# A graph recommender on one core: SyncE and ScalarE gather row by row one tile in two rounds instead of one in each

## The chip, the cores and the metric

The kernel runs on one core of a Trainium2 chip. The metric is the device time of one execution in microseconds, the median over several runs; lower is better. The engines are TensorE (PE), VectorE (DVE), ScalarE (ACT), GpSimd (POOL) and SyncE (SP), each with its own instruction queue; they meet by semaphores.

## The reference, cut to what matters

The graph has 12,501 nodes with rows of 128 float32 (`emb`) and 150,000 edges (row, column, value).

```python
h = emb
acc = emb
for _ in range(2):
    h = segment_sum(adj_val[:, None] * h[adj_col], adj_row, num_segments=N)
    acc = acc + h
graph_item_embs = acc / 3
combined = graph_item_embs[items] + item_features[items]
# 512 sessions of 50 items: gather through alias_inputs, two small products with tanh
# and sigmoid, a weighted sum per session, normalized: select (512 x 128)
scores = select @ l2norm(graph_item_embs).T          # 512 x 12501
```

The part around the change is `h[adj_col]`: for each of two layers, one row of 512 bytes is fetched from HBM for each edge.

## The kernel before, in words

**Sorting.** A first stage sorts the edges by buckets of 256 target nodes into a table in HBM (`sorted_edges`), padded so that each tile of 128 edges belongs to one bucket. There are NU = 1244 tiles.

**A layer.** For every tile, 128 rows of the source (`emb` in layer 0, `table1` in layer 1) are gathered into one slot of `msg`, one row per partition. VectorE writes a one-hot matrix of 128 x 256 with the edges' values (L1118), TensorE multiplies it with the gathered rows (L1444), and VectorE adds the result to the bucket's columns of `acc` in SBUF (L1167). The one-hot is made LEAD = 4 tiles ahead.

**Rounds.** The tiles go in rounds of T = 24: NST = 52 rounds, numbered c = 0 to 51, the last with 20 tiles. `msg` holds two rounds, h = c % 2. Before a round, ScalarE copies its 24 columns of metadata into small buffers (`fetch`, L660 to L662) once the matmuls of round c - 2 are done; the last of the copies releases GpSimd's gathers of that round.

**Who gathers.** GpSimd issues one indirect DMA for each tile (L574), in order of the tiles; at tiles 0, 8 and 16 of a round it waits until the matmul of 12 tiles earlier is done (PACE = 8, AHEAD = 12). The last tile of the rounds 1 to 49 (`is_own`, NOWN = 49 in each layer) is left out there: SyncE and ScalarE gather it row by row, 64 rows each. For each half of 32 rows they load 32 byte offsets into registers (L442, L682), and for each row issue one copy of 512 bytes (L446, L686), each with a MOVE before it. All 128 rows count on one semaphore (`s_line`), which VectorE waits for before the one-hot of that tile and then clears. The offsets stand in `own_at`, which VectorE prepares from the sorted edges before the layers.

**Order on ScalarE.** In layer 0, for each round: fetch(c), then its 64 rows of the last tile of round c. In layer 1: wait for TensorE's transposes of embeddings, two copies (L710, L711) that TensorE's next transposes (L1438) need, fetch(c + 2), then the 64 rows of round c + 2. On SyncE: a wait for the matmuls that free the slot, then the 64 rows.

**After.** Between the layers `acc` is transposed and written to HBM as `table1`; after layer 1 the session part follows, with 200 indirect gathers by GpSimd and the 512 x 12501 scores.

Of the kernel before, what the change touches and what calls it, by code (L numbers as in the profile page):

```python
# [38 lines left out]
def recommender_program(nc, items, inputs, alias, features, adj_row, adj_col, adj_val, emb,  # L39
# [34 lines left out]
    T = 24  # L74

    NT = -(-((E + GR * NB * (R - 1) + NB * (P - 1)) // P) // T) * T
    NST = NT // T
# [2 lines left out]
    PACE, AHEAD = 8, 12  # L80
    LINE = 4 * D
    HALF, AT_ONCE = P // 2, 32
    NOWN = NST - 3
    M = 4
    NU = -(-((E + GR * NB * (R - 1) + NB * (P - 1)) // P) // M) * M
    PER = NU // M
# [18 lines left out]
    FITS = "a tile's offset is 256 times the buckets that begin at or before it, less one: 0 to ROWS - 256"  # L105

    def is_own(j):
        return j % T == T - 1 and 1 <= j // T <= NOWN

    FED = [sum(1 for j in range(u, NU, 2 * T) if not is_own(j)) for u in range(2 * T)]  # L110

# [2 lines left out]
    with ExitStack() as ctx:  # L114
# [55 lines left out]
        at[0] = -(-NT // P) * 2 * P  # L170
        own_lines = carve(big, NOWN * HALF * 2)[0:2, :].rearrange("o (k s w) -> o k s w", k=NOWN, w=2)
        assert at[0] <= ROWS
# [57 lines left out]
        block_at_l = carve(stage, NKL * P)  # L230
        own_at = stage[0:2, 6 * D:6 * D + NOWN * HALF].bitcast(I32)
        assert 6 * D + NOWN * HALF <= 4 * 512 * 2
        assert at[0] <= 4 * 512 * 2
# [107 lines left out]
        s_lines = sem("s_lines")  # L341
# [4 lines left out]
        s_mm = [sem(f"s_mm{m}") for m in range(M)]  # L346
# [52 lines left out]
        emb_bytes = emb.rearrange("n d -> (n d)").bitcast(U8)  # L399
        table1_bytes = table1.rearrange("n d -> (n d)").bitcast(U8)  # L400
# [15 lines left out]
        @block.sync  # L416
        def _(sp):
            sp.wait_ge(s_init, 3)
            for n, (dst, src) in enumerate(((e_row, adj_row), (e_col, adj_col), (e_val, adj_val))):
                sp.dma_start(dst[:, 0:COLS], src[0:COLS * P].rearrange("(p t) -> p t", t=COLS)).then_inc(s_edge, 16)  # L420
                sp.dma_start(dst[0:TAIL, COLS:COLS + 1],
                             src[COLS * P:E].rearrange("(p t) -> p t", t=1)).then_inc(s_edge, 16)
            sp.wait_ge(s_blank, 2)
            sp.dma_start(slots.rearrange("(p x) w -> p (x w)", p=P), blank.rearrange("p x w -> p (x w)")).then_inc(s_zero, 16)

            sp.wait_ge(s_free, GR + 3)
            lines = slots.rearrange("(j x) w -> j (x w)", x=P // R)
            full = NT // P
            sp.dma_start(big[:, 0:2 * P], lines[0:P, :]).then_inc(s_meta0, 16)
            sp.dma_start(big[:, 2 * P:full * 2 * P].rearrange("p (m w) -> p m w", m=full - 1),  # L430
                         lines[P:full * P, :].rearrange("(m p) w -> p m w", p=P)).then_inc(s_meta, 16)
            sp.dma_start(big[0:NT - full * P, full * 2 * P:(full + 1) * 2 * P], lines[full * P:NT, :]
                         ).then_inc(s_meta, 16)
            for half in range(2):
                sp.dma_start(own_lines[half:half + 1].rearrange("o k s w -> o k (s w)"),
                             lines[T:T * (NOWN + 1), 2 * HALF * half:2 * HALF * (half + 1)
                                   ].rearrange("(k t) w -> t k w", t=T)[T - 1:T]).then_inc(s_lines, 16)

            def own_rows(source, first, h):

                for a in range(0, HALF, AT_ONCE):
                    _, starts = nc.values_load_multi_w_load_instructions(  # L442
                        own_at[0:1, bass.ds(first + a, AT_ONCE)], engines=[mybir.EngineType.SP],
                        min_val=0, max_val=LINE * (N - 1), skip_runtime_bounds_check_because=HELD)
                    for p, begin in enumerate(starts):
                        sp.dma_start(msg_bytes[h][a + p:a + p + 1, :],  # L446
                                     source[bass.ds(begin, LINE)].rearrange("(o b) -> o b", o=1)).then_inc(s_line[h], 16)

            def own_tiles(layer, source):

                own_rows(source, 0, 1)
                with sp.Fori(1, NST // 2 - 1) as i:
                    for h in range(2):
                        sp.wait_ge(s_mm[M - 1], i * (2 * T // M) + (PER * layer + T // M * (h - 1)))
                        own_rows(source, i * (2 * HALF) + HALF * (h - 1), h)

            sp.wait_ge(s_mrdy, 3)
            own_tiles(0, emb_bytes)

            for r in range(NB // GRP):  # L460
                sp.wait_ge(s_t1a, (GRP * (r + 1) + 1) // 2)
                sp.wait_ge(s_t1v, (GRP * (r + 1)) // 2)
                a, b = 2 * GRP * r, 2 * GRP * (r + 1)
                sp.dma_start(tab[0][:, a:b, :], big_rows[:, a:b, :]).then_inc(s_t1w, 16)
            sp.wait_ge(s_t1w, 16 * (NB // GRP))

            sp.dma_start(big_rows[:, 0:emb_full, :],
                         emb[0:emb_full * P, :].rearrange("(g p) d -> p g d", p=P)).then_inc(s_eld, 16)
            sp.wait_ge(s_fz, 1)
            sp.dma_start(big_rows[0:emb_rest, emb_full, :], emb[emb_full * P:N, :]).then_inc(s_eld, 16)  # L470

            own_tiles(1, table1_bytes)

            sp.wait_ge(s_ec, NB)
            sp.dma_start(big_rows[0:emb_rest, emb_full, :], features[emb_full * P:N, :]).then_inc(s_fld, 16)
            sp.dma_start(big_rows[:, 0:emb_full, :],
                         features[0:emb_full * P, :].rearrange("(g p) d -> p g d", p=P)).then_inc(s_fld, 16)
            for r in range(NB // GRP):
                sp.wait_ge(s_cmb, GRP * (r + 1))
                a, b = 2 * GRP * r, 2 * GRP * (r + 1)  # L480
                sp.dma_start(tab[1][:, a:b, :], ring_rows[:, a:b, :]).then_inc(s_cw, 16)

            for bt in range(BT):
                for q in range(-(-NS // 2)):
                    m = (-(-NS // 2)) * bt + q
                    sp.wait_ge(s_sca, m + 1)
                    if 2 * q + 1 < NS:
                        sp.wait_ge(s_scv, (NS // 2) * bt + q + 1)
                    a, b = 1024 * q, min(1024 * q + 1024, N)
                    sp.dma_start(out[bt * P:(bt + 1) * P, a:b], ostage[:, m % 4, 0:b - a]).then_inc(s_out[m % 4], 16)  # L490
            total = (-(-NS // 2)) * BT
            for i in range(4):
                sp.wait_ge(s_out[i], 16 * ((total - i + 3) // 4))
# [109 lines left out]
        def _(act):  # L603
# [63 lines left out]
            for m in range(-(-NT // P)):  # L667
                w = min(P, NT - P * m)
# [10 lines left out]
            def own_rows(source, first, h):  # L679

                for a in range(0, HALF, AT_ONCE):
                    _, starts = nc.values_load_multi_w_load_instructions(  # L682
                        own_at[1:2, bass.ds(first + a, AT_ONCE)], engines=[mybir.EngineType.Activation],
                        min_val=0, max_val=LINE * (N - 1), skip_runtime_bounds_check_because=HELD)
                    for p, begin in enumerate(starts):
                        act.dma_start(msg_bytes[h][HALF + a + p:HALF + a + p + 1, :],  # L686
                                      source[bass.ds(begin, LINE)].rearrange("(o b) -> o b", o=1)).then_inc(s_line[h], 16)
# [3 lines left out]
            with act.Fori(1, NST // 2 - 1) as i:  # L691
                for h in range(2):
                    fetch(0, 2 * i + h, h)
                    own_rows(emb_bytes, i * (2 * HALF) + HALF * (h - 1), h)
            for c in range(NST - 2, NST):
                fetch(0, c, c % 2)

# [15 lines left out]
            with act.Fori(0, LOOP // 2) as i:  # L713
                for h in range(2):
                    emb_rows(2 * i + h, h)
                    fetch(1, 2 * i + h + 2, h)
                    own_rows(table1_bytes, i * (2 * HALF) + HALF * (h + 1), h)
            for c in range(LOOP, max(NB, NST - 2)):
                if c < NB:
                    emb_rows(c, c % 2)  # L720
# [74 lines left out]
        def _(dve):  # L795
# [301 lines left out]
            for m in range(-(-NT // P)):  # L1097
                w = min(P, NT - P * m)
# [9 lines left out]

            def one_hot(layer, it, u):

                if u % T < T - 1:
                    dve.wait_ge(s_g[u], 16 * (FED[u] * layer + it + 1))
                elif isinstance(it, int) and not is_own(2 * T * it + u):
                    dve.wait_ge(s_g[u], 16 * (FED[u] * layer + (FED[u] if it else 1)))
                else:
                    dve.wait_ge(s_line[u // T], 16 * P)
                    dve.sem_clear(s_line[u // T])
                dve.tensor_scalar(onehot[:, u % SR, :], bank[7][:, 0:BUCKET], mlo[:, u:u + 1], mval[:, u:u + 1],  # L1118
                                  ALU.is_equal, ALU.mult).then_inc(s_S[u % M], 1)
# [469 lines left out]
```

## Time and profile before

| | us |
|---|---|
| median of 3 runs | 4178.22 |
| lowest, highest | 4175.29, 4179.51 |
| profiled execution, span | 6020.2 |
| busy in it: PE, DVE, POOL | 3070.2, 3014.4, 2890.1 |
| busy in it: PEld, ACT | 1849.5, 866.4 |

The profile shows one execution, with the hardware's recorder of instructions on; for it no time other than the span is given. Its span is 1842 us longer than the median of the runs, which are made without the recorder. Rows of the profile are those of this longer execution. Time that an engine's queue spends on issuing a DMA, on register moves and on loads of registers is not in its busy time; the rows name such a queue with a q (ACTq, SPq).

### The profile page before, as it was taken

To read this page: it belongs to the slowest core of one execution; us is meant where nothing else is said; L and a number is where in the kernel's file an instruction comes from. 1 tells how busy PE (TensorE), PEld (TensorE's weight loads), DVE (VectorE), ACT (ScalarE), POOL (GpSimd) and SP (SyncE) were. 2 spreads that over 40 slices of the span, in tenths; PEclk is the share of its full clock that TensorE was granted. 3 is DMA by queue.
4 is the path that set the end of the run, shared out by engine and by line. 5 is a ranking of instruction groups with operands and counts; after the bars stand their busy time and mean duration, and the time that the engine had idled before them with its cause. 6 is when DMAs were issued, how large, how long until landed. Compare 5 with 4: busy or idle time off the path is not lost.

```text
span 6020.2 us, 68764 instructions
## 1 busy us (share of the span) xinstructions
PE 3070.2 (51%) x9778; PEld 1849.5 (31%) x9778; DVE 3014.4 (50%) x7257; ACT 866.4 (14%) x3005; POOL 2890.1 (48%) x2965
## 2 busy tenths in 40 slices
PE   5988744444444444444444444444444444445578
PEld 3777622222222222222222222222222222222344
DVE  8999754444444444444444444444444444445455
ACT  2998800000000000000000000000000000000543
POOL 1666654444444444444445454454454454455561
PEclk8888866666666666666666666666666666666689
DMA  0000011111111111111114111111111111112454
GB/s 25 4 3 3 3 48 33 32 31 32 32 31 33 33 34 33 34 33 31 32 32 120 34 37 35 33 37 36 32 37 35 33 37 35 34 36 80 79 84 139
DMA packets 162229, 235.35 MB, mean 39 GB/s; under 512 B 67554, under 2 KB 107776, under 8 KB 161952
## 3 DMA queue, kind: packets, MB, share of 16 engines
q0 software_dynamic: 92896, 171.14, 12.4%
q1 hardware_dynamic: 54132, 58.90, 3.0%
q10 hardware_dynamic: 15052, 3.83, 0.3%
q14 instruction: 118, 0.97, 0.1%
q8 instruction: 31, 0.51, 0.0%
HBM read 192.69 MB, written 41.01 MB: 39 GB/s over the span
## 4 chain that ended last, share of the span: by engine, by line
ACTq 49%; issue 32%; DVE 7%; PE 6%; ACT 3%; another core or an unknown queue 2%; POOL 1%; DMA 0%; DVEq 0%; SPq 0%; POOLq 0%
ACTq L686 43%; ACTq L682 5%; ACT big L644 2%; PE bank L1520 1%; PE bank L1382 1%; POOL sorted_edges L542 1%; DVE stage L944 1%; PE bank L1548 1%; DVE acc L1167 1%; DVE big L888 1%; PE bank L1507 1%; DVE ring L896 0%; PE bank L1482 0%; DVE big L904 0%
## 5 line engine op out<-in xcount | busy, mean ns | idle before, releaser
L1444 PE MATMUL bank<-ring 128*128 128x256 f32 x4976 | 2105.7, 558 | 2135.8 <-DVE ring L1118 1194.1
L1444 PEld LDWEIGHTS bank<-ring 128*128 128x128 f32 x4976 | 1147.7, 263 | 3071.0 <-DVE ring L1118 1662.5
L574 POOL DMA_INDIRECT ring<-in_L_rec_emb,cring x1195 | 1134.9, 950 | 1336.2 <-ACT cring L662 978.9
L1167 DVE TENSOR_TENSOR acc<-acc,bank 128x256 f32 x2488 | 1029.6, 414 | 1481.3 <-remote 1131.6
L1118 DVE TENSOR_SCALAR ring<-bank,mlo,mval 128x256 f32<-128x256 f32 x2488 | 1343.5, 540 | 742.4 <-DMA ring<-in_L_rec_emb 523.1
L574 POOL DMA_INDIRECT ring<-table,cring x1195 | 1130.2, 946 | 1202.8 <-PE bank L1444 795.7
L644 ACT ACTIVATE big<-big 128x68 f32<-128x68 bf16 x1764 | 557.7, 405 | 1.2 <-issue 1.2
L1382 PE MATMUL bank<-big,ring 128*128 128x136 f32 x2352 | 430.8, 328 | 75.5 <-issue 20.8
L542 POOL DMA_INDIRECT sorted_edges<-moved,block_to x313 | 397.2, 1269 | 100.3 <-issue 100.0
L1382 PEld LDWEIGHTS bank<-big,ring 128*128 128x128 f32 x2352 | 356.8, 219 | 147.6 <-ACT big L644 83.2
L660 ACT COPY mlo<-ring 128x24 f32 (+1 forms) x104 | 21.7, 209 | 2415.0 <-issue 2381.6
L710 ACT COPY idle<-ones 128x1 f32<-128x1 f32 x49 | 9.4, 192 | 2191.6 <-issue 2191.6
L1438 PE MATMUL bank<-ident,stage 128*128 128x128 f32 x98 | 33.7, 448 | 524.7 <-ACT stage L711 524.7
L597 POOL DMA_INDIRECT ring<-combined,sidi x200 | 190.5, 952 | 156.6 <-issue 56.0
L1148 DVE TENSOR_TENSOR acc<-acc,bank 128x256 f32 (+1 forms) x49 | 20.6, 421 | 468.1 <-PE bank L1438 468.1
L1438 PEld LDWEIGHTS bank<-ident,stage 128*128 128x128 f32 x98 | 14.2, 204 | 556.9 <-ACT stage L711 556.9
L896 DVE TENSOR_TENSOR ring<-bank,place_p 128x1024 f32<-128x1024 f32 x147 | 178.7, 1215 | 7.0 <-remote 4.1
L1520 PE MATMUL bank<-acc,big 128*128 128x512 f32 (+1 forms) x200 | 104.7, 635 | 5.5 <-ACT big L754 3.5
L888 DVE TENSOR_TENSOR big<-bank,place_c 128x544 bf16<-128x544 f32 x147 | 105.4, 717 | 0.3
L1391 PE MATMUL bank<-dsnow,ring 50*128 50x1 f32 x626 | 98.6, 288 | 0.0
L1391 PEld LDWEIGHTS bank<-dsnow,ring 50*128 50x128 f32 x626 | 96.9, 244 | 2.5
L904 DVE TENSOR_TENSOR big<-big 128x272 f32<-128x272 bf16 x147 | 92.8, 632 | 0.0
(213 smaller groups left out, 1700.7 us busy)
## 6 DMA issues: line engine op xcount, KB each, us to landing
ring<-in_L_rec_emb SPq DMA_DIRECT2D x3136, 0.5 KB
ring<-in_L_rec_emb ACTq DMA_DIRECT2D x3136, 0.5 KB
ring<-table ACTq DMA_DIRECT2D x3136, 0.5 KB
ring<-table SPq DMA_DIRECT2D x3136, 0.5 KB
scores<-stage SPq DMA_DIRECT2D x48, 512.0 KB
ring<-in_L_rec_emb,cring POOLq DMA_INDIRECT x1195
ring<-table,cring POOLq DMA_INDIRECT x1195
table<-big SPq DMA_DIRECT2D x7, 896.0 KB, 9.1
```

Of the source, the lines that this page charges most:

```text
L542: pool.indirect_dma_start(slots, bass.IndirectOffsetOnAxis(block_to[:, h, k:k + 1], 0), moved[:, h, (skip + k) * R:(skip + k + 1) * R, :]. ...
L574: pool.indirect_dma_start(msg[:, s, :], None, source, bass.IndirectOffsetOnAxis(cring[:, s:s + 1], 0)).then_inc(s_g[s], 16)
L597: pool.indirect_dma_start(seq[:, half, l, :], None, combined, bass.IndirectOffsetOnAxis(sidi[:, l, bt:bt + 1], 0)).then_inc(s_sq[half * NG ...
L644: last = act.activation(at_c[:, r, t, q, :], hot_c[:, r, :, t], ACT.Copy, scale=what[:, bass.ds(n * C + t, 1)])
L682: _, starts = nc.values_load_multi_w_load_instructions(own_at[1:2, bass.ds(first + a, AT_ONCE)], engines=[mybir.EngineType.Activation], mi ...
L686: act.dma_start(msg_bytes[h][HALF + a + p:HALF + a + p + 1, :], source[bass.ds(begin, LINE)].rearrange("(o b) -> o b", o=1)).then_inc(s_li ...
L896: dve.tensor_tensor(at_p[:, r, :, :], row_p.unsqueeze(1).broadcast_to([P, C, P]), place_p[:, h, s * C:(s + 1) * C].unsqueeze(2).broadcast_ ...
L1118: dve.tensor_scalar(onehot[:, u % SR, :], bank[7][:, 0:BUCKET], mlo[:, u:u + 1], mval[:, u:u + 1], ALU.is_equal, ALU.mult).then_inc(s_S[u ...
L1167: add = dve.tensor_tensor(acc[:, bass.ds(off, BUCKET)], acc[:, bass.ds(off, BUCKET)], bank[u % PR][:, 0:BUCKET], ALU.add)
L1382: last = pe.matmul(group_bank(h)[:, 0:2 * LC], at_p[:, r, t, :], at_c[:, r, t, :, :].rearrange("p w c -> p (w c)"), start=(s == 0 and t == ...
L1391: last = pe.matmul(bank[7][:, k:k + 1], begun[0:NB + 1, k * P:(k + 1) * P], dsnow[:, :], start=True, stop=True)
L1444: pe.matmul(bank[u % PR][:, 0:BUCKET], msg[:, h * T + u, :], onehot[:, u % SR, :], start=True, stop=True).then_inc(s_mm[u % M], 1)
```

## The change

The row-by-row tile becomes the last tile of every second round: tiles 47, 95, ... in place of 47, 71, 95, .... NOWN goes from 49 to 25 in each layer; the rounds 1, 3, ..., 49 keep theirs, and the last tiles of the rounds 2, 4, ..., 48 are gathered by GpSimd like all others. The loops of SyncE and ScalarE issue their 64 rows once for two rounds, after the fetch of the odd one, and always into the slot of h = 1. VectorE's wait for the other slot's last tile becomes the ordinary one. `FED`, which counts GpSimd's gathers per slot, follows from `is_own`.

```diff
-    NOWN = NST - 3
+    NOWN = NST // 2 - 1
...
     def is_own(j):
-        return j % T == T - 1 and 1 <= j // T <= NOWN
+        return j % (2 * T) == 2 * T - 1 and j // (2 * T) < NOWN
...
                 sp.dma_start(own_lines[half:half + 1].rearrange("o k s w -> o k (s w)"),
-                             lines[T:T * (NOWN + 1), 2 * HALF * half:2 * HALF * (half + 1)
-                                   ].rearrange("(k t) w -> t k w", t=T)[T - 1:T]).then_inc(s_lines, 16)
+                             lines[0:2 * T * NOWN, 2 * HALF * half:2 * HALF * (half + 1)
+                                   ].rearrange("(k t) w -> t k w", t=2 * T)[2 * T - 1:2 * T]).then_inc(s_lines, 16)
...
                 own_rows(source, 0, 1)
                 with sp.Fori(1, NST // 2 - 1) as i:
-                    for h in range(2):
-                        sp.wait_ge(s_mm[M - 1], i * (2 * T // M) + (PER * layer + T // M * (h - 1)))
-                        own_rows(source, i * (2 * HALF) + HALF * (h - 1), h)
+                    sp.wait_ge(s_mm[M - 1], i * (2 * T // M) + PER * layer)
+                    own_rows(source, i * HALF, 1)
...
             with act.Fori(1, NST // 2 - 1) as i:
                 for h in range(2):
                     fetch(0, 2 * i + h, h)
-                    own_rows(emb_bytes, i * (2 * HALF) + HALF * (h - 1), h)
+                own_rows(emb_bytes, i * HALF, 1)
...
                 for h in range(2):
                     emb_rows(2 * i + h, h)
                     fetch(1, 2 * i + h + 2, h)
-                    own_rows(table1_bytes, i * (2 * HALF) + HALF * (h + 1), h)
+                own_rows(table1_bytes, i * HALF + HALF, 1)
...
             def one_hot(layer, it, u):
 
-                if u % T < T - 1:
+                if u < 2 * T - 1:
                     dve.wait_ge(s_g[u], 16 * (FED[u] * layer + it + 1))
```

## Rows read from the trace of the kernel before

**Rows 1.** The page: span, busy time, DMA queues, chain that ended last

```profile
span 6020.2 us, 68764 instructions
...
PE 3070.2 (51%) x9778; PEld 1849.5 (31%) x9778; DVE 3014.4 (50%) x7257; ACT 866.4 (14%) x3005; POOL 2890.1 (48%) x2965
...
q1 hardware_dynamic: 54132, 58.90, 3.0%
q10 hardware_dynamic: 15052, 3.83, 0.3%
...
ACTq L686 43%; ACTq L682 5%; ACT big L644 2%; PE bank L1520 1%; PE bank L1382 1%; POOL sorted_edges L542 1%; DVE stage L944 1%; PE bank L1548 1%; DVE acc L1167 1%; DVE big L888 1%; PE bank L1507 1%; DVE ring L896 0%; PE bank L1482 0%; DVE big L904 0%
```

**Rows 2.** Timeline of ScalarE: start us, us, what; stalled, clean, second layer

```profile
3073.15 25.99 ACTq L686 DMA_DIRECT2D ring<-in_L_rec_emb  x12
...
3104.38 10.35 ACTq L686 DMA_DIRECT2D ring<-in_L_rec_emb  x32
3114.93 0.21 ACT L660 COPY mlo<-ring 128x24 f32 x1 [48.49 <-issue]
3115.05 0.21 ACT L661 COPY mval<-ring 128x24 f32 x1
3115.16 0.20 ACT L662 COPY cring<-ring 128x24 int32 x1
...
4537.02 1.19 ACTq L686 DMA_DIRECT2D ring<-table  x4
4538.25 0.19 ACT L710 COPY idle<-ones 128x1 f32<-128x1 f32 x1 [43.80 <-issue]
4538.36 0.41 ACT L711 COPY stage<-big 128x256 f32 x1
...
4541.08 9.65 ACTq L686 DMA_DIRECT2D ring<-table  x21
```

**Rows 3.** Lines 686, 682, 446 in short stretches: ns min/median/max, first and last

```profile
L686 ACTq MOVE ring<-in_L_rec_emb x12: 4/353/692, 3072.4 to 3097.7; - x12
...
L686 ACTq MOVE ring<-in_L_rec_emb x30: 29/29/29, 3104.3 to 3113.8; - x30
L686 ACTq DMA_DIRECT2D ring<-in_L_rec_emb x30: 228/229/462, 3104.4 to 3113.9; - x30
...
L682 ACTq TENSOR_LOAD <-stage x1: 2148/2148/2148, 3102.1 to 3102.1; - x1
...
L446 SPq MOVE ring<-in_L_rec_emb x13: 632/691/708, 3071.8 to 3098.4; - x13
L446 SPq DMA_DIRECT2D ring<-in_L_rec_emb x12: 5/694/701, 3072.4 to 3097.7; - x12
...
L446 SPq DMA_DIRECT2D ring<-in_L_rec_emb x3136: 3/225/1399, 775.5 to 3165.8; - x196
```

**Rows 4.** Timeline of GpSimd across the end of round 49, first layer

```profile
3138.15 0.94 POOL L574 DMA_INDIRECT ring<-in_L_rec_emb,cring  x1 [0.30 <-issue]
...
3143.15 0.94 POOL L574 DMA_INDIRECT ring<-in_L_rec_emb,cring  x1 [0.30 <-issue]
3163.84 0.95 POOL L574 DMA_INDIRECT ring<-in_L_rec_emb,cring  x1 [19.75 <-ACT cring L662]
```

**Rows 5.** Waits, whole span: us in total, times, longest us

```profile
POOL ring L574 <- ACT cring L662: 978.9, 50, 20.8
...
PE bank L1438 <- ACT stage L711: 524.7, 49, 15.9
```

**Rows 6.** Timeline of VectorE, nothing late: first and last of five tiles

```profile
3051.75 0.54 DVE L1118 TENSOR_SCALAR ring<-bank,mlo,mval 128x256 f32<-128x256 f32 x1
...
3055.66 0.54 DVE L1118 TENSOR_SCALAR ring<-bank,mlo,mval 128x256 f32<-128x256 f32 x1
```

**Rows 7.** Timeline of GpSimd: first gather, between the layers, last gather

```profile
756.38 0.98 POOL L574 DMA_INDIRECT ring<-in_L_rec_emb,cring  x1 [4.38 <-ACT cring L662]
...
3222.23 0.95 POOL L574 DMA_INDIRECT ring<-in_L_rec_emb,cring  x1 [0.30 <-issue]
3262.57 0.95 POOL L574 DMA_INDIRECT ring<-table,cring  x1 [39.38 <-DMA table<-big]
...
5555.23 0.95 POOL L574 DMA_INDIRECT ring<-table,cring  x1 [0.30 <-issue]
```

## The prediction, made before the changed kernel was run

> **What bounds the kernel now.** I started from the engines' busy times and the chain that ended last [rows 1]. The reader is to see two things. No engine is over 51% busy, and the chain lies 43% on L686 and 5% on L682, which are ScalarE's queue issuing single rows. And the span, 6020.2 us, is 1842 us longer than the 4178.22 us that the runs without the recorder take. A page that is 44% too long can name a bound that the timed runs don't have, so the first question is where the 1842 us lie.
>
> The views of ScalarE's queue answer it. In one stretch a half of 32 rows goes out in 10.35 us [rows 2] with its load of 2.15 us before it [rows 3]; in another, some 30 us earlier, 12 rows take 25.99 us [rows 2], a MOVE of a register between them takes up to 0.69 us where it otherwise takes 0.029, and SyncE's MOVEs and DMAs take 0.69 us in the same stretch [rows 3]. A MOVE issues no transfer. When it stretches on two engines at once, the thing that is slow is not the row transfer; I take it for the recording of the instructions, which the timed runs don't do. The pitch without these stalls is (10.35 - 0.46) / 31 = 0.319 us a row, 0.46 being the longest issue, the first after the load [rows 2, 3].
>
> From that follows ScalarE's round without stalls: a half is 2.15 + about 0.09 + 10.35 = 12.6 us, two are 25.2, and the fetch takes 3115.36 - 3114.73 = 0.63 us plus some 0.2 of the loop: 26.0 us a round [rows 2, 3]. In the second layer two more copies (L710, L711) come before the fetch: 4541.08 - 4538.21 = 2.87 us from row to row, load included, instead of 2.15 + 0.09 = 2.24, and the two copies are 0.1 to 0.4 us long; I take 26.4 there [rows 2]. SyncE has the same 64 issues, with 0.225 us in place of 0.229 each, and no fetch [rows 3].
>
> GpSimd gives the other side. Its gathers come at 1.251 us (3143.15 - 3138.15 over 4 steps), 0.95 us busy and 0.30 of gap, and then it waits 19.75 us for the fetch that ScalarE's stalled queue holds back [rows 4]. Without that wait a round of 23 gathers is 23 x 1.251 = 28.8 us. That is 2.4 to 2.8 us more than ScalarE's clean round. The rest is faster: VectorE turns a tile over in 0.78 us when nothing is late (3055.66 - 3051.75 over 5 tiles), 18.8 us a round [rows 6].
>
> Check by the sum. Outside the two gather stages lie 756.4 us before the first gather, 39.1 us between the layers (the 39.38 less the ordinary 0.30), and 6020.2 - 5555.2 - 1.25 = 463.7 us at the end: 1259.2 us [rows 1, 7]. With GpSimd as the only bound the kernel takes 1259.2 + 2 x 1195 x 1.251 = 4249 us. With ScalarE's clean rounds as the only bound it takes 1259.2 + 49 x 26.0 + 49 x 26.4 + 170 (two times 68 gathers of rounds that have no row-by-row tile) = 3997 us. The median of 4178.22 lies 181 us above the second and 71 us under the first, and 71 us is just 0.030 us per gather. So I read the timed runs as bound by GpSimd at (4178.2 - 1259.2) / 2390 = 1.221 us per gather, with the recorder costing the other 0.03. The difference in level is taken up by this: the span itself is no base for the sum, the median is.
>
> **The change part by part.**
>
> *Gathers added.* Row-by-row tiles fall from 49 to 25 in each layer, so GpSimd issues 24 more gathers per layer, 48 in all: 1195 become 1219 twice. Each is a gather on the engine that I hold for the bound. From below it costs 0.95 us (only the busy part, if the gap could be covered), from above 1.251 us (the pitch seen); I take 1.221. Sum: 48 x 1.221 = +58.6 us, bounds +45.6 and +60.0.
>
> *Row transfers removed.* 24 x 64 x 2 = 3072 issues go from each of SyncE and ScalarE, with 96 loads of 2.15 us. That frees ScalarE about 24 x 25.2 = 605 us per layer. It is worth nothing if its round lay 2 us under GpSimd's. The cover that hides it today is the row of gathers; if that cover is missing, the freed time is the gain of the first rival.
>
> *Lateness of the rows that stay.* They are issued after the fetch of the odd round, which waits on the same matmuls that free the slot, nearly two rounds before the tile is turned over. Clean, 25.2 us of issues stand against some 50 us. Behind them in ScalarE's queue stand the next fetch and, in the second layer, the copies L710 and L711, for which TensorE's transposes (L1438) wait. Today that is so every round, hereafter every second; it costs nothing new. In the profiled execution the queue will still stall, so some of TensorE's wait for L711 will be seen there.
>
> *Set-up.* The list of row addresses shrinks from 49 x 64 to 25 x 64; the three small VectorE steps on it (L1105 to L1107) get a few us shorter while GpSimd already gathers. They lie on nothing that ends last: taken as 0, with at most 5 us gained. VectorE's wait on the line semaphore and its clearing fall away 48 times in all and are replaced by the ordinary wait: 0.
>
> *Fewer transfers in flight.* The two hardware queues together, with everything else on them, take 3.3% of the DMA engines' span [rows 1], and GpSimd's gap of 0.30 us is the same beside rows in flight and after the last of them [rows 4, 7]. Taken as 0.
>
> **A rule that speaks for a gain.** ScalarE's issue is 0.229 us in the rows [rows 3]. The Trainium skill, page "DMA: Bandwidth & Descriptors", in the table that closes the section "Why a DMA increments its semaphore by 16 and not by 1", gives 512 sequencer cycles for a copy instruction of the earlier generations, and "Advanced Engine Details and Errata", section "Clock Domains", 1.2 GHz for the sequencers: 0.427 us each. By that rule, as an estimate, ScalarE's round would be 64 x 0.427 + 2 x 2.24 + 0.8 = 32.6 us, more than GpSimd's, the kernel before would take over 4600 us and the change would bring it down to the gathers' time. The trace does not agree: 0.229 us stands against 0.427, and the median of before is far under 4600. Its result is B below, in a stronger form.
>
> **The rivals.**
>
> *A, likeliest: GpSimd is the bound.* 1259.2 + 2438 x 1.221 = 4236.8, or 4178.2 + 58.6: **4237 us**. Chance 0.86. Own range 4215 to 4245, from the bounds of the price, the set-up, and the spread of the three runs (4.2 us).
>
> *B: ScalarE's queue bounds the timed runs too.* It needs (4178.2 - 1259.2 - 170) / 98 = 28.05 us a round, 2 us over the clean one, which is 0.03 us more per row than the trace's best. Then the gather pitch is unknown and lies somewhere under 1.221. The change is a gain from the point where it is under (4178.2 - 1259.2) / 2438 = 1.197 us. The recorder's share would be the one thing that makes the pitch smaller: if three recorded steps of 0.03 us were in a gather, it would be 1.16 us, and the time 1259.2 + 2438 x 1.16 = 4087 us. For it: the chain, and GpSimd's 978.9 us of waits for ScalarE [rows 1, 5]. Against it: the MOVEs of 0.69 us, and that 71 us fit one such step per gather. Chance 0.08.
>
> *C: both queues about equal.* Between them, with a gather of 1.19 to 1.20 us in the timed runs, gain and loss cancel: 1259.2 + 2438 x 1.197 = 4178 us. The two rounds are 2.4 us apart in the rows, which leaves room for it only if each is off. Chance 0.04.
>
> *D: a new wait.* In the second layer TensorE waits for L711 until ScalarE has issued a full tile (524.7 us of waits, with the stalls [rows 5]). Should the pile-up of one tile in every second round reach GpSimd's gathers (which stop when the matmuls lag by more than 12 to 20 tiles), 24 waits of 1 to 2 us come on top: 4260 to 4285, say 4272. Clean, the copies are due about 30 us after the issues begin, and a lag of under 10 us reaches no gather. Chance 0.02.
>
> **How the numbers follow.** Slower by over 0.2% (8 us, about what a measurement of this kernel can tell from no change) is A and D: 0.88. Same is C with a little of B: 0.04. Faster is B: 0.08. The range 4212 to 4248 holds about 0.93 of A and nothing of the others, 0.80 in all; it is A's own range, drawn a little wider.
>
> **What the profile of the changed kernel would show.** GpSimd with 1219 gathers twice and at the same 0.95 us; rows issued 1600 times per engine and layer; GpSimd's waits for the fetch nearly gone and the chain on GpSimd's gathers (or their gaps) instead of L686. Its span should fall far, to 1259 + 2438 x 1.251 = 4309 us plus what stalls are left, say 4310 to 4450, though the timed runs get slower. A median under 4170 would mean that the timed runs were bound by ScalarE's issues, and that the fastest pitch in the trace is not the pitch without the recorder. A median over 4250 would point to waits that the gathers run into.

## The result, and the profile after

The changed kernel takes **4235.46 us** (median of 4 runs, 4233.24 to 4237.0) against 4177.4 us (4 runs, 4175.29 to 4179.51): 58.1 us or 1.4% more, ratio 1.014 with the 95% interval 1.0126 to 1.0155. The forecast was 4237 us, slower.

The page of the changed kernel (its lines are one lower than those of before from L574 on: GpSimd's gather is L573, ScalarE's row L685, TensorE's product L1443):

```profile
span 4235.2 us, 56068 instructions
...
PE 3245.6 (77%) x9778; PEld 1823.8 (43%) x9778; DVE 3090.9 (73%) x7257; ACT 870.0 (21%) x3005; POOL 2928.7 (69%) x3013
...
q10 hardware_dynamic: 8908, 2.25, 0.3%
...
POOL ring L573 26%; POOL ring L596 2%; DMA scores<-stage 2%; PE bank L1519 1%; PE bank L1481 1%; PE bank L1547 0%; DMA ring<-table,cring 0%; PE bank L1472 0%; DMA ring<-combined,sidi 0%; PE bank L1506 0%; ACT stage L731 0%; ACT acc L725 0%; DMA table<-big 0%; PE bank L1488 0%; ACT big L742 0%
```

Beside [rows 1] the reader is to see that ScalarE's queue has left the chain and GpSimd's gathers are its largest part, and that this span, 4235.2 us, agrees with the timed runs, while the first profile of before is 1842 us above its own. A comparison of the two pages would call this change a gain of 30%.

The groups of the gathers, with what ended GpSimd's idle time before them, in the changed kernel:

```profile
L573 POOL DMA_INDIRECT ring<-in_L_rec_emb,cring x1219 | 1152.4, 945 | 376.0 <-issue 370.9 <-ACT cring L661 4.5 <-PE bank L1443 0.6
L573 POOL DMA_INDIRECT ring<-table,cring x1219 | 1150.2, 944 | 403.6 <-issue 369.6 <-DMA table<-big 32.1 <-PE bank L1443 1.8
```

GpSimd waits 4.5 us for ScalarE instead of the 978.9 of [rows 5], and nothing else of size but the wait for the table between the layers interrupts it. That is one engine at its own pace for 3046 us of 4235.

**The same kernel before, profiled again.** Because the first profile of before didn't fit its times, the unchanged kernel was profiled once more, and two further profiles with the same number of instructions came by the way (e2 and e3, below).

> The kernel before, unchanged, profiled once more. If the 6020 us of its first profile belong to the kernel under the recorder, the span is again near 6020 us, with MOVEs of up to 0.7 us on SyncE and ScalarE. If they belonged to that one execution, the span is 4171 to 4179 us as in the profiles of the runs that issue the same number of instructions (68764), with a pitch of 1.25 us for GpSimd's gathers and ScalarE waiting 2 to 3 us a round for the matmuls.

Measured: span 4178.4 us, time 4180.22 us. Its page, the gathers, and ScalarE's rows between 900 and 2200 us:

```profile
span 4178.4 us, 68764 instructions
...
POOL ring L574 24%; DMA ring<-table,cring 3%; PE bank L1520 2%; POOL ring L597 1%; DMA scores<-stage 1%; DMA ring<-combined,sidi 1%; PE bank L1444 1%; PE bank L1548 1%; PE bank L1482 1%; PE bank L1507 0%; DVE ring L1118 0%; PE bank L1473 0%; PE bank L1489 0%; ACT stage L732 0%; ACT acc L726 0%
```

```profile
L574 POOL DMA_INDIRECT ring<-in_L_rec_emb,cring x1195 | 1135.1, 950 | 369.2 <-issue 355.3 <-PE bank L1444 9.5 <-ACT cring L662 4.4
L574 POOL DMA_INDIRECT ring<-table,cring x1195 | 1130.1, 946 | 396.9 <-issue 354.3 <-DMA table<-big 32.2 <-PE bank L1444 10.4
```

```profile
L686 ACTq MOVE ring<-in_L_rec_emb x2816: 29/29/29, 901.0 to 2161.9; - x188
L686 ACTq DMA_DIRECT2D ring<-in_L_rec_emb x2816: 228/229/542, 901.0 to 2162.0; - x188
```

The long MOVEs of [rows 3] are not there, nor is the wait of [rows 4]. The 6020 us were those of one execution. Neither the kernel as such nor the recording of it takes that long. This profile is the one that the changed kernel's is to be compared with.

GpSimd's timeline at the ends of the stages, kernel before (again) and changed kernel:

```profile
742.98 0.99 POOL L574 DMA_INDIRECT ring<-in_L_rec_emb,cring  x1 [4.40 <-ACT cring L662]
...
2241.88 0.94 POOL L574 DMA_INDIRECT ring<-in_L_rec_emb,cring  x1 [0.31 <-issue]
2275.06 0.94 POOL L574 DMA_INDIRECT ring<-table,cring  x1 [32.23 <-DMA table<-big]
...
3768.91 0.95 POOL L574 DMA_INDIRECT ring<-table,cring  x1 [0.30 <-issue]
```

```profile
743.09 0.98 POOL L573 DMA_INDIRECT ring<-in_L_rec_emb,cring  x1 [4.45 <-ACT cring L661]
...
2266.02 0.94 POOL L573 DMA_INDIRECT ring<-in_L_rec_emb,cring  x1 [0.30 <-issue]
2299.09 0.94 POOL L573 DMA_INDIRECT ring<-table,cring  x1 [32.13 <-DMA table<-big]
...
3819.78 0.94 POOL L573 DMA_INDIRECT ring<-table,cring  x1 [0.30 <-issue]
```

With one pitch of 1.25 us for the last gather, the stages last 1500.2 + 1495.1 = 2995.3 us before and 1524.2 + 1521.9 = 3046.1 us after: 50.8 us more. Start (743.0 and 743.1) and the time between the layers are equal; the part after the last gather is 408.3 and 414.2 us. It varies between 405.7 and 414.2 us over all profiles of this case but the first, whatever the kernel (406.3 in e10, which is the changed kernel with smaller loads), so of the 56.8 us between these two spans some 6 are chance. The profile of before with the shortest stages (e3, below) has 2990.4 us. The change thus costs 51 to 56 us in the stages; what it is made of stands behind the experiments.

### The profile page after: what moved, and what is told of

The parts are those of the page before. It is cut to its first block and busy times, and to the rows that moved or that the text cites. A ratio compares the mean times of both kernels' runs of the same rounds, so it can differ in the third digit from the quotient of the medians.

```text
span 4235.2 us, 56068 instructions
## 1 busy us (share of the span) xinstructions
PE 3245.6 (77%) x9778; PEld 1823.8 (43%) x9778; DVE 3090.9 (73%) x7257; ACT 870.0 (21%) x3005; POOL 2928.7 (69%) x3013
## 5 line engine op out<-in xcount | busy, mean ns | idle before, releaser
L1443 PE MATMUL bank<-ring 128*128 128x256 f32 x4976 | 2290.4, 585 | 759.2 <-DVE ring L1117 724.8
L1443 PEld LDWEIGHTS bank<-ring 128*128 128x128 f32 x4976 | 1126.2, 267 | 1898.1 <-DVE ring L1117 1847.6
L573 POOL DMA_INDIRECT ring<-table,cring x1219 | 1150.2, 944 | 403.6 <-issue 369.6
L573 POOL DMA_INDIRECT ring<-in_L_rec_emb,cring x1219 | 1152.4, 945 | 376.0 <-issue 370.9
L1381 PE MATMUL bank<-big,ring 128*128 128x136 f32 x2352 | 439.8, 325 | 59.6 <-DVE ring L895 15.8
L1310 DVE COPY stage<-bank 128x512 f32<-128x512 f32 x48 | 33.1, 690 | 64.6 <-PE bank L1519 38.2
L1296 DVE TENSOR_TENSOR big<-bank,big 128x512 f32<-128x512 f32 (+1 forms) x52 | 34.8, 670 | 57.7 <-PE bank L1547 57.7
```

The lines of the kernel that those rows point to most:

```text
L573: pool.indirect_dma_start(msg[:, s, :], None, source, bass.IndirectOffsetOnAxis(cring[:, s:s + 1], 0)).then_inc(s_g[s], 16)
L1381: last = pe.matmul(group_bank(h)[:, 0:2 * LC], at_p[:, r, t, :], at_c[:, r, t, :, :].rearrange("p w c -> p (w c)"), start=(s == 0 and t == ...
L1443: pe.matmul(bank[u % PR][:, 0:BUCKET], msg[:, h * T + u, :], onehot[:, u % SR, :], start=True, stop=True).then_inc(s_mm[u % M], 1)
```

## The experiments

Theory A: GpSimd's gathers bound both kernels, and ScalarE's and SyncE's rows lie beside them with 2 to 3 us to spare in each round. Theory B, the rival: the queue that issues the rows bounds the kernel before. All edits but e10's are to the kernel before, whose runs on the same chip stand beside each.

**e1: the rows taken away.** From the loops of SyncE and ScalarE the issues are gone; VectorE waits for round 1's rows alone.

```diff
-                    own_rows(emb_bytes, i * (2 * HALF) + HALF * (h - 1), h)
...
-                    own_rows(table1_bytes, i * (2 * HALF) + HALF * (h + 1), h)
...
-                else:
+                elif isinstance(it, int) and it == 0:
                     dve.wait_ge(s_line[u // T], 16 * P)
```

> The kernel before without the row-by-row transfers of rounds 2 to 49 in each layer: SyncE and ScalarE issue only the rows of round 1, and VectorE doesn't wait for the others, so those tiles are multiplied with rows that an earlier round left. GpSimd's 1195 gathers a layer stay. Theory A (GpSimd's gathers, at 1.248 us each in the profile after, are the bound and the rows are free): no change, 4177 +- 8 us. Theory B (ScalarE's queue is the bound in the timed runs): the rows go from the path and the time falls below 4100 us.

Measured: 4174.33 us against 4175.45; ratio 0.9997 (0.9988 to 1.0007). This kernel leaves 12,288 row transfers out, and they are worth nothing. That alone decides against B, and against any gain by less traffic.

**e4: all rows by GpSimd.** `is_own` is false for every tile, and SyncE and ScalarE issue no rows.

> All tiles gathered by GpSimd, no rows at all: 98 gathers more than before, 50 more than after. A: each costs its pitch of 1.248 us, 4177.4 + 98 x 1.248 = 4299.7 us; with the 1.221 us of the prediction 4297, with the busy part alone (0.944 us) 4270. B: 98 x its pitch more, less what the rows cost: under 4250 us.

Measured: 4295.64 us against 4175.45, 120.2 us more; ratio 1.0288 (1.0271 to 1.0305). That is 1.23 us for each of 98 gathers, where the change has 58.1 / 48 = 1.21. By the interval the 98 cost 113 to 127 us, so this confirms a linear price near the pitch, and excludes the busy part alone (4270 us). It can't tell 1.221 from 1.248.

**e2 and e3: an added load, which was not there.** One or two more register loads behind the rows of each round, on ScalarE:

```diff
                     own_rows(emb_bytes, i * (2 * HALF) + HALF * (h - 1), h)
+                    nc.values_load_multi_w_load_instructions(
+                        own_at[1:2, 0:AT_ONCE], engines=[mybir.EngineType.Activation],
+                        min_val=0, max_val=LINE * (N - 1), skip_runtime_bounds_check_because=HELD)
```

> The kernel before with one more load of 32 registers (2.15 us, with its setting 2.2) in ScalarE's queue behind the rows of each of 98 rounds. A: ScalarE's round of 26.0 to 26.4 us goes to 28.2 to 28.6, still just under GpSimd's 23 x 1.248 = 28.7: 4177 to 4187 us. B: every round is 2.2 us longer, 4177 + 98 x 2.2 = 4393 us.

> The same with two loads (4.5 us) a round. A: ScalarE's rounds of 30.5 and 30.9 us are now the bound, 1.8 and 2.2 us over GpSimd's: 4177 + 49 x 4.0 = 4373 us. B: 4177 + 98 x 4.5 = 4618 us. What this run takes over one load alone places the slack of ScalarE's queue without the recorder.

Measured: 4176.4 and 4173.67 us against 4175.45. The second contradicts A's 4373 us, until one reads the trace of e3:

```profile
span 4171.5 us, 68764 instructions
...
L682 ACTq TENSOR_LOAD <-stage x196: 2114/2154/2309, 759.2 to 3672.5; - x196
```

196 loads and 68764 instructions are those of the kernel before: loads whose values nobody uses were not built. Neither run says anything on the slack. Their traces, though, are further profiles of the kernel before, with one round of ScalarE (timeline, e3):

```profile
1904.70 0.21 ACT L660 COPY mlo<-ring 128x24 f32 x1 [28.49 <-PE bank L1456]
1904.82 0.21 ACT L661 COPY mval<-ring 128x24 f32 x1
1904.93 0.21 ACT L662 COPY cring<-ring 128x24 int32 x1
1907.22 23.36 ACTq L686 DMA_DIRECT2D ring<-in_L_rec_emb  x64
1933.29 0.21 ACT L660 COPY mlo<-ring 128x24 f32 x1 [28.15 <-PE bank L1456]
```

From one fetch to the next are 28.59 us. The rows end at 1930.58, 25.9 us after the first copy, and for the next 2.7 us the queue waits for the matmuls. That is the round of 26.0 us that the prediction worked out from the stretches without stalls, and the slack that A needs.

**e5, e6, e9: a real load on the queues.** The offsets are loaded 8, 4 and 16 at a time instead of 32:

```diff
-    HALF, AT_ONCE = P // 2, 32
+    HALF, AT_ONCE = P // 2, 8
```

> The kernel before with its row offsets loaded 8 at a time instead of 32 (8 loads a round on SyncE and on ScalarE instead of 2). The trace has 2.15 us for a load of 32 values and none of another size: between a quarter of it (then nothing changes) and all of it (then 8 x 2.2 = 17.6 us in place of 4.5, and a round of 39 us). A: ScalarE has 2.7 us of slack a round; the time is 1187 + the larger of the two queues' rounds, so 4176 us if a load of 8 costs under 0.9 us, and 98 x (8 x load - 7.2) more if it costs more. B: every microsecond that the loads add counts from the first one on, 98 us of time for each.

> The same with 4 at a time, 16 loads a round. If a load has a fixed part of about 0.6 us, 16 of them take some 13 us with the offsets in place of 4.5, a round on ScalarE is 34 to 35 us. A: 98 x (34.5 - 28.7) = +570 us, near 4750 us; the profile's own load time must give the measured time through 98 x (round - 28.7). B: 98 x 8.5 = +830 us.

> The kernel before with the offsets loaded 16 at a time, 4 loads a round in place of 2. By the loads of 32, 8 and 4 (2.15, 0.75, 0.51 us) one of 16 takes 1.2 us, and with what stands around each (some 0.35 us) the round of SyncE and ScalarE grows by about 1.3 us. A (GpSimd's gathers bound, ScalarE waits 2.2 to 3.1 us a round for the matmuls): all of it lies in that wait, 4178 +- 8 us. B (ScalarE's queue bounds): 98 x 1.3 = +127 us, 4305 us.

Measured: with 16 at a time 4174.43 us against 4175.5 (0.9987 to 1.0006), with 8 4354.89 against 4178.16 (1.0356 to 1.0454), with 4 4911.53 against 4178.16 (1.1749 to 1.1789). The loads in the three traces, e9, e5 and e6 (first and last start after the nanoseconds):

```profile
L682 ACTq TENSOR_LOAD <-stage x392: 1187/1222/1466, 758.5 to 3675.8; - x196
```

```profile
L682 ACTq TENSOR_LOAD <-stage x784: 717/750/897, 759.3 to 3870.2; - x196
...
POOL ring L574 <- ACT cring L662: 134.2, 44, 4.8
POOL ring L574 <- PE bank L1444: 73.4, 63, 2.1
```

```profile
L682 ACTq TENSOR_LOAD <-stage x1568: 478/512/770, 759.1 to 4427.2; - x196
...
POOL ring L574 <- ACT cring L662: 384.5, 48, 10.1
```

The first step is free, as A says and B doesn't (4305 us). A's size for e5 was wrong: by the load's 0.75 us it should have stayed free. Two costs were left out. The first row after each load takes 0.46 to 0.54 us instead of 0.23 ([rows 3], and the maximum in the line of L686 above), eight times a round instead of twice. And at the end of the loop's body, once in two rounds of the first layer, 2.9 us pass between the last row (1482.06) and the fetch, with nothing waited for, where e8 below has 0.5; in e5's second layer it is about 0.6 us. Why the longer body has this gap was not found. ScalarE's timeline in e5, first layer:

```profile
1477.80 4.26 ACTq L686 DMA_DIRECT2D ring<-in_L_rec_emb  x9
1484.99 0.21 ACT L660 COPY mlo<-ring 128x24 f32 x1 [32.67 <-issue]
```

So the queue's round was past GpSimd's (from fetch to fetch 31.6 us on average in the first layer of e5 and 30.2 in the second, against 28.7), and from there on the time follows it. GpSimd now waits for the fetch again: 134.2 + 73.4 us for the fetch and for matmuls that are late behind it, where the kernel before has 24.3 for both, against 177 us of time. What B asks for, 98 us of time for each microsecond of a round from the first on, doesn't hold below the crossing, and nearly holds past it: e6, with 36.7 us from fetch to fetch and 8.0 over GpSimd's round, took 733 / 98 = 7.5 us a round more than before. Its forecast of 570 us was too low by the same two costs.

**e10: the same load on the changed kernel.**

> The changed kernel with the offsets loaded 8 at a time, which cost the kernel before 177 us. A: with rows in every second round only, ScalarE has a whole round to spare and nothing changes against the changed kernel: 4235 +- 8 us, so the order of the two reverses, 4235 against 4355. B: the loads count in each of 50 rounds with rows, 4235 + 90 = 4325 us.

Measured: 4230.71 us; ratio to before 1.0135 (1.0118 to 1.0152), where the changed kernel has 1.014. With rows in every second round the queue has more than a round to spare, and what cost 177 us costs nothing. ScalarE's timeline in the changed kernel shows it: the rows end at 1948.96, and the next fetch comes 5.2 us later. No rows follow that fetch, and the one after it comes 27.4 us later.

```profile
1923.02 0.21 ACT L659 COPY mlo<-ring 128x24 f32 x1 [27.33 <-PE bank L1443]
...
1925.55 23.41 ACTq L685 DMA_DIRECT2D ring<-in_L_rec_emb  x64
1954.18 0.21 ACT L659 COPY mlo<-ring 128x24 f32 x1 [30.72 <-PE bank L1443]
...
1981.60 0.21 ACT L659 COPY mlo<-ring 128x24 f32 x1 [26.99 <-PE bank L1443]
```

**e8: gathers taken away instead.**

```diff
+    def is_left(j):
+        return 2 <= j // T <= 49 and 18 <= j % T <= 22
...
-                    if is_own(T * c + u):
+                    if is_own(T * c + u) or is_left(T * c + u):
```

> The kernel before without GpSimd's gathers of the tiles 18 to 22 of the rounds 2 to 49 (5 x 48 x 2 = 480 gathers less); those tiles are multiplied with rows that an earlier round left. A: GpSimd's round falls to 18 x 1.248 = 22.5 us and ScalarE's queue becomes the bound at 26.0 to 26.4: 2.3 to 2.7 us a round less than 28.7, 4176 - 96 x 2.5 = 3936 us and not the 480 x 1.248 = 599 us that the gathers would be worth. B: 4176 us, no change.

Measured: 3910.86 us against 4178.16; ratio 0.9364 (0.9348 to 0.9379), 267 us less. Taking gathers away helps at once, which B denies, and stops being worth anything at ScalarE's round. Its timeline there:

```profile
1022.33 0.21 ACT L663 COPY mlo<-ring 128x24 f32 x1 [25.58 <-issue]
...
1024.87 23.15 ACTq L689 DMA_DIRECT2D ring<-in_L_rec_emb  x64
1048.55 0.21 ACT L663 COPY mlo<-ring 128x24 f32 x1 [25.78 <-issue]
```

The fetches come 26.2 us apart, with nothing waited for between the rows and the fetch ("issue" in place of the product). The forecast for this run was 3936 us, 25 more than measured. It left out that ScalarE starts each layer ahead of GpSimd: by the starts of GpSimd's first gathers, the first four shortened rounds of the first layer and the first two of the second take 22.5 us, GpSimd's own pace, and only then do the rounds rise to 26.

**e7: what a gather is paid for.**

```diff
-                    pool.indirect_dma_start(msg[:, s, :], None, source,
-                                            bass.IndirectOffsetOnAxis(cring[:, s:s + 1], 0)).then_inc(s_g[s], 16)
+                    n = P if c < 2 else HALF
+                    pool.indirect_dma_start(msg[0:n, s, :], None, source,
+                                            bass.IndirectOffsetOnAxis(cring[0:n, s:s + 1], 0)).then_inc(s_g[s], 16)
```

> The kernel before with 64 rows instead of 128 in each of GpSimd's gathers from round 2 on; the other half of each tile keeps what earlier rounds left. It asks what a gather's 1.248 us are paid for. If for the instruction, nothing changes: 4176 us. If the busy part (0.944) halves, GpSimd's round is 23 x 0.78 = 18 us, ScalarE's 26.0 to 26.4 become the bound, and 98 x (28.7 - 26.2) = 245 us go: 3930 us. B: no change, since ScalarE bounds already.

Measured: 4076.3 us against 4178.16; ratio 0.9757 (0.974 to 0.9773), 101.9 us less. The group in its trace:

```profile
L575 POOL DMA_INDIRECT ring<-in_L_rec_emb,cring x1195 | 1086.1, 909 | 368.8 <-issue 356.4 <-PE bank L1445 7.9 <-ACT cring L663 4.5
```

Half the rows cost 0.909 instead of 0.950 us, 4% less, and over 2390 gathers that is the gain (2390 x 0.041 = 98 us). Between 64 and 128 rows a gather is paid by the instruction and hardly by its rows. Rows shifted from GpSimd to the other queues are thus worth much only when a whole gather goes, and the 2.7 us of slack in a round hold, as an estimate, 7 more rows on ScalarE's queue (2.7 less 0.51 for a load, at 0.319 a row). No version that beats the kernel before came out of this, and none was run.

## Why the prediction was right, and where it was not

*The bound.* Right, and shown. The 1842 us between span and times were rightly taken as no part of the timed runs, ScalarE's clean round of 26.0 us is that of the undisturbed trace (25.9), and the gathers bound the kernel (e1, e4, e8). Rivals B, C and D are excluded: B by e1, e8 and e9; C by e9, where 1.3 us more a round on both row queues cost nothing, and by the pitch of 1.25 us; D by 2.4 us of waits for the product in the changed kernel, in both layers together. The same 2.4 us answer a rival that the prediction doesn't name, slower matmuls: TensorE's granted clock was 0.74 in the runs of the changed kernel against 0.76 in those of the kernel before, but GpSimd hardly ever waited for a product.

*The price of a gather.* 1.221 us was taken, and the change cost 58.1 / 48 = 1.21. But the step that led there, "the recorder costing the other 0.03", was wrong: in three profiles of the kernel before whose spans (4171.5 to 4178.4 us) agree with the times, and in that of the changed kernel, the pitch is 1.25 us as in [rows 4]. What was 71 us too long in the sum of 4249 us lay outside the gathers: 743 us in place of 756.4 at the start, 31.9 in place of 39.1 between the layers, 408 in place of 463.7 at the end, 1183 in place of 1259.2 us. With these, 1183 + 2390 x 1.25 = 4171 us. An assumption spread over the wrong rows gave nearly the right price by luck. The price of a gather is its full pitch. By the starts of the first gather of each round, the rounds of the changed kernel with 23 gathers take 28.7 us and those with 24 take 30.0, in both layers from the second round to the last full one: 1.25 us for the one more, and 60 us for 48.

*The set-up.* It was taken as 0, with at most 5 us gained, and it is what takes the 60 us down. The three VectorE steps on the list of row addresses run while GpSimd does its first gathers, and the gathers beside them take longer. Kernel before (again) and changed kernel, first step, last step, and the longest gather beside them:

```profile
753.81 1.77 DVE L1105 CAST stage<-big 2x3136 int32<-2x3136 f32 x1
756.02 3.33 POOL L574 DMA_INDIRECT ring<-in_L_rec_emb,cring  x1 [0.30 <-issue]
757.44 1.78 DVE L1107 TENSOR_SCALAR stage<-stage 2x3136 int32<-2x3136 int32 x1
```

```profile
752.95 0.99 DVE L1104 CAST stage<-big 2x1600 int32<-2x1600 f32 x1
753.46 1.62 POOL L573 DMA_INDIRECT ring<-in_L_rec_emb,cring  x1 [0.30 <-issue]
754.99 0.98 DVE L1106 TENSOR_SCALAR stage<-stage 2x1600 int32<-2x1600 int32 x1
```

With the shorter list the first round of the first layer takes 31.8 us (32.1 in e10). It takes 34.2 to 34.6 in every later profile with the long list, e1 without rows and e4 without row-by-row tiles among them. So the change is worth 60 less about 2.5, or 57.5 us, against 58.1 measured (53 to 65 by the interval). The forecast's 58.6 had 1.4 us too little for the gathers and these 2.5 us too much: two small errors that nearly cancel. The 51 to 56 us of the stages lie a little lower because the mean pitch differs between profiles of the kernel before (1.249 to 1.252 us in the rounds 2 to 49), and 0.003 us over 2390 gathers are 7 us.

*The cause of the stalls.* The prediction took the long MOVEs for the recording of instructions, "which the timed runs don't do". That recording by itself stretches the queues is refuted: the same 68764 instructions were recorded without a stall. What stretched that one execution stays open.

*The rows taken away, the lateness of the rest, fewer transfers.* Each was costed at 0, and e1 and e10 agree. TensorE's wait for L711, 524.7 us in [rows 5], is gone in the profile after, where the prediction expected some of it to be left, and is 0.2 us in the later profile of before.

*The rule that speaks for a gain.* The Trainium skill, page "DMA: Bandwidth & Descriptors", section "Why a DMA increments its semaphore by 16 and not by 1", gives 512 sequencer cycles per copy, from which the prediction estimated over 4600 us. The trace doesn't agree: the issues take 0.229 us in the undisturbed profiles too.

*What the profile was to show.* 1219 gathers twice, 1600 rows per engine and layer, waits for the fetch gone: as forecast. The span of 4310 to 4450 us was not: it is 4235.2. That error is the one above: the stretching was thought to belong to every profiled execution.

## What to carry to other kernels

When a profile's span is far from the kernel's times, profile again before reading a bound from it; until then, take each engine's pace from its stretches without stalls, see which sum reproduces the time, and don't put a remainder on one of its terms without a reason: the stages outside the gathers were stretched too. Moving work from a bound engine to others pays until their own round is as long, and not a step further; here 128 rows in every round fitted with 2.7 us to spare, and giving up every second one cost the 48 gathers that came back, less 2.5 us of set-up. A test load has to survive into the program: count the instructions in its trace before believing that it cost nothing.

## What had not been expected of the hardware

One execution of the kernel before took 6020 us, with register MOVEs of up to 0.7 us on SyncE and ScalarE at once, where three others of the same instructions took 4171 to 4178 us. A load of registers costs 0.51, 0.75, 1.22 and 2.15 us for 4, 8, 16 and 32 values, which a fixed 0.27 and 0.06 for each value fit. Beside three small VectorE steps of 1.8 us on two partitions a gather of GpSimd took 3.33 instead of 0.95 us; beside steps of 1.0 us the longest took 1.62. An indirect gather of 64 rows of 512 bytes keeps GpSimd only 4% less busy than one of 128 rows.
